# Delta-rule steps of a vision tower: two half-width read sums joined into one

## The chip, the cores and the metric

The kernel runs on one core of a Trainium2 chip. It is written instruction by instruction: each of TensorE (PE), VectorE (DVE), ScalarE (ACT), GpSimd (POOL) and the queue of SyncE (SP) has its own program, and semaphores order them against each other. The metric is the device time of one execution in microseconds, taken as the median of several.

## The reference

The model is a vision tower of four blocks over 32 images of 64 tokens with 256 features. The change lies in the attention of the second block, a gated delta rule with 16 heads of 16 features, which runs over the 64 tokens one after the other:

```
q = silu(x @ Wq); k = silu(x @ Wk); k = k * rsqrt(sum(k * k, -1) + 1e-12); v = x @ Wv
beta = 2 * sigmoid(x @ Wbet); a = sigmoid(x @ Wf)
def step(S, inp):                                   # S: 16 x 16 for each image and head
    qt, kt, vt, at, bt = inp
    Sd = at[..., None, None] * S
    u = vt - einsum('bhk,bhkv->bhv', kt, Sd)
    Sn = Sd + bt[..., None, None] * kt[..., None] * u[:, :, None, :]
    o = einsum('bhk,bhkv->bhv', qt, Sn)
    return Sn, o
```

Every state needs the one before it. There are 32 x 16 = 512 independent chains of 64 steps. Patch embedding, an attention, a mixture of experts, a channel mixer, a causal attention, grouped experts, a linear recurrence and an int8 projection surround it; the change leaves them alone.

## The kernel before

The 512 chains are laid out as 128 partitions (8 images x 16 heads) by 4 groups `g`. A state is 4 x 16 x 16 = 1024 f32 values on each partition, two PSUM banks. Two copies, `S[0]` (banks 0 and 1) and `S[1]` (banks 2 and 3), are used in turn. `halves[h]` cuts the four groups into two halves of 512 values, one bank each. The loop over `t` is written once on each engine, in `delta_layer`:

- DVE (`vector`, lines 1608 to 1623) does for half 0 and then for half 1: the product of the state with the scaled key (`prod`, line 1613), its sum over the 16 keys (`read`, line 1616), the subtraction from the value (`u`, line 1619), and the outer product of the scaled key with `u` (`outer`, line 1622). `prod` and `outer` lie in the tile that the trace calls `made`; `read` and `u` lie in PSUM bank 4. All four are written for both halves before the next `t` begins.
- ACT (`scalar`, from line 1511) waits for `prod_made{h}` and fades the state of half h into the other copy with two instructions (line 1517, `faded{h}`). It then copies the present state of that half to SBUF for the output (`copy_out`, line 1494). After both halves it stores an earlier output (line 1498).
- PE (`add_outer`, line 1411) waits for `faded{h}` and `outer_made{h}` and adds the outer product to the faded state with a matmul by the identity; the semaphore `state{h}` tells DVE that this half of the next state is there. After both halves PE sums the folded output products of step t - 2 (`sum_folded`, line 1419, four matmuls of 64 columns), and sometimes squares (line 1426).
- POOL (`gpsimd`, from line 1669) multiplies the copied state with the query for the output (line 1674) and folds it twice (line 1678). It waits for both copies of a step (`state_copied`).

An f32 matmul shows in the trace as two MATMUL instructions, so a "pair" below is one call of `add_outer` for one half.

The loop keeps two things going at once: while PE adds the outer product of one half, DVE works on the other half. The wait that joins them is this one, at the head of each half:

```
dve.wait_ge(sem(f"state{h}"), t + 1)
```

Nothing else in the block is queued behind the loop until it ends. Its last output, a short tail of normalisation, and the loads for the next layers follow.

Of the kernel before, what the change touches and what calls it, by code (L numbers as in the profile page):

```python
# [13 lines left out]
ALU = mybir.AluOpType  # L14
ACT = mybir.ActivationFunctionType
AX = mybir.AxisListType
# [57 lines left out]
def bcast(ap, axis, n):  # L74

    ap = ap.unsqueeze(axis)
    shape = [int(s) for s in ap.shape]
    shape[axis] = n
    return ap.to_broadcast(shape)
# [1172 lines left out]
def delta_layer(nc, sem, io, banks, H, ident, minus_half, token_rows, gate, chains, rates, front, chain, all_sent,  # L1252
# [15 lines left out]
    q, k, v, o = (chain[n] for n in "qkvo")  # L1268
    ka, kb, qt = (chain[n] for n in ("ka", "kb", "q_by_time"))
    rate, n2, rn, tmp, f = (chain[n] for n in ("rate", "n2", "rn", "rn_tmp", "f"))  # L1270
    states = "p n m -> p (n m)"

    def by_state(ap):
        return ap.rearrange("p (g v k) -> p g v k", g=CG, v=HD)

    Sc = [by_state(xT[i][:, :, :].rearrange(states)) for i in range(2)]
    prod, outer = (by_state(made_all[:, 2 * i:2 * i + 2, :].rearrange(states)) for i in range(2))
# [10 lines left out]
    read, u = small[:, 0, :, :], small[:, 1, :, :]  # L1288
    halves = [slice(2 * h, 2 * h + 2) for h in range(2)]
# [249 lines left out]
    def vector(dve):  # L1539
# [68 lines left out]
        for t in range(TOK):  # L1608
            now = slice(t, t + 1)
            for h in range(2):  # L1610
                at = halves[h]
                dve.wait_ge(sem(f"state{h}"), t + 1)
                dve.tensor_tensor(prod[:, at, :, :], S[t % 2][:, at, :, :], bcast(ka[:, t, at, :], 2, HD),  # L1613
                                  ALU.mult).then_inc(sem(f"prod_made{h}"), 1)
                dve.wait_ge(sem(f"prod_made{h}"), t + 1)
                dve.tensor_reduce(read[:, at, :], prod[:, at, :, :], AX.X, ALU.add  # L1616
                                  ).then_inc(sem(f"read_made{h}"), 1)
                dve.wait_ge(sem(f"read_made{h}"), t + 1)
                dve.tensor_tensor(u[:, at, :], v[:, at, :, now].rearrange("p g d o -> p g (d o)"),
                                  read[:, at, :], ALU.subtract).then_inc(sem(f"u_made{h}"), 1)  # L1620
                dve.wait_ge(sem(f"u_made{h}"), t + 1)
                dve.tensor_tensor(outer[:, at, :, :], bcast(kb[:, t, at, :], 2, HD), bcast(u[:, at, :], 3, HD),  # L1622
                                  ALU.mult).then_inc(sem(f"outer_made{h}"), 1)
        for n in range(CHUNKS_O - 1):
# [19 lines left out]
    def gpsimd(pool):  # L1644
# [24 lines left out]
        for t in range(TOK - 1):  # L1669
# [7 lines left out]
            for i, n in enumerate((8, 4)):  # L1677
                pool.tensor_tensor(qs[:, :, :, 0:n], qs[:, :, :, 0:n], qs[:, :, :, n:2 * n],  # L1678
                                   ALU.add).then_inc(sem("qs_folded"), 1)
                pool.wait_ge(sem("qs_folded"), 2 * t + i + 1)  # L1680

    return {"early_loads": early_loads, "sync": sync, "tensor": tensor, "scalar": scalar, "vector": vector,
            "gpsimd": gpsimd}

# [1012 lines left out]
```

## Time and profile before

| | |
|---|---|
| median of 3 runs | 1444.47 us (1439.58 to 1448.13) |
| profiled execution, its time | 1432.16 us |
| its span, first to last instruction | 1430.5 us |
| busy in the span: PE / DVE / ACT / POOL | 80% / 58% / 40% / 40% |
| mean granted TensorE clock | 0.917 of full speed |
| loop over the tokens | from 679.6 us to about 976 us of the span |

Busy shares are over the whole span, which has stages with quite different limits. The loop is one of these stages, a fifth of the time. In it no DMA of any size runs, and what matters is how the four engines pass a state round within a step.

### The profile page before, as it was taken

Reading aid. Unit: us, or ns where it says so; the run is one execution under the profiler, and the core shown is the slowest. Engines: PE = TensorE matmul, PEld = TensorE weight load, DVE = VectorE, ACT = ScalarE, POOL = GpSimd, SP = SyncE. Lnnn points to the kernel's source line nnn. Section 1 sums busy time; section 2 is a strip of 40 time slices with the busy share of each in tenths; the row PEclk is TensorE's granted clock in tenths of the full one; section 3 lists DMA queues with packets and bytes.
Section 4 is the critical chain, followed back from the end, with each engine's and each line's share of the span. In section 5 each row is a group of like instructions: output and inputs, shape, how many; then the busy total and the mean of one; then the engine's idle time right before and its main releaser. Section 6 shows DMA issues by size and latency. Waiting matters only on the chain. (4 is left out here: it accounts for less than half of the span.)

```text
span 1430.5 us, 24008 instructions
## 1 busy us (share of the span) xinstructions
PE 1137.5 (80%) x8723; PEld 838.7 (59%) x8723; DVE 833.5 (58%) x1982; ACT 565.7 (40%) x1340; POOL 566.3 (40%) x626
## 2 busy tenths in 40 slices
PE   5999984699999999686776777764899999776843
PEld 3666663687988889532333444442677777654532
DVE  3666665311121211455999999996477777522875
ACT  1455541211111112154566666662234443334643
POOL 0111111232323333343799999994121122120756
PEclk9999995799999999799799999997799999978975
DMA  4111100788888887387000000002000040037501
GB/s 133 42 45 35 42 13 17 302 332 341 318 300 316 307 312 269 98 220 179 0 0 1 0 1 0 1 1 74 12 12 9 9 185 2 1 123 250 170 12 49
DMA packets 83349, 162.19 MB, mean 113 GB/s; under 512 B 44128, under 2 KB 62176, under 8 KB 77216
## 3 DMA queue, kind: packets, MB, share of 16 engines
q1 hardware_dynamic: 55536, 111.23, 22.6%
q0 software_dynamic: 10512, 45.10, 8.7%
q10 hardware_dynamic: 17184, 4.33, 1.4%
q8 instruction: 71, 1.16, 0.3%
q14 instruction: 46, 0.38, 0.1%
HBM read 134.28 MB, written 26.35 MB: 112 GB/s over the span
## 5 line engine op out<-in xcount | busy, mean ns | idle before, releaser
L1411 PE MATMUL banks<-made,ident 128*128 128x512 f32 x256 | 151.1, 674 | 90.4 <-DVE made L1622 89.6
L908 PE MATMUL banks<-rowsT,w_up 128*128 128x128 f32 x1716 | 199.8, 276 | 0.7 <-DMA w_up<-in_up_w 0.7
L908 PEld LDWEIGHTS banks<-rowsT,w_up 128*128 128x128 f32 x1716 | 196.4, 193 | 1.3 <-DMA w_up<-in_up_w 1.0
L1674 POOL TENSOR_TENSOR ys<-xT_d,q_by_time 128x1024 f32<-128x1024 f32 x63 | 148.8, 2361 | 17.9 <-ACT xT_d L1494 9.8
L1517 ACT ACTIVATE banks<-banks,rate 128x256 f32<-128x256 f32 x256 | 104.1, 445 | 116.5 <-DVE made L1613 116.5
L1411 PEld LDWEIGHTS banks<-made,ident 128*128 128x128 f32 x256 | 40.9, 201 | 154.2 <-ACT banks L1517 128.2
L1678 POOL TENSOR_TENSOR ys<-ys 128x512 f32<-128x512 f32 x126 | 124.8, 990 | 9.9
L923 PE MATMUL banks<-w_down,hT 128*128 128x256 f32 x468 | 115.1, 388 | 0.6 <-DVE res L1092 0.6
L1082 DVE TENSOR_TENSOR hT<-banks,silu 64x128 f32<-64x128 f32 x39 | 11.0, 283 | 170.7 <-ACT silu L966 170.7
L852 POOL DMA_DIRECT2D w_down<-in_down_w x39 | 22.8, 584 | 195.2 <-PE banks L923 190.1
L1821 POOL TENSOR_TENSOR agg_b<-agg_b,minus_half 128x1 f32<-128x1 f32 x48 | 28.5, 593 | 171.1 <-DVE agg_b L2031 169.9
L923 PEld LDWEIGHTS banks<-w_down,hT 128*128 128x128 f32 x468 | 82.6, 189 | 22.0 <-issue 13.9
L1419 PEld LDWEIGHTS banks<-ys,ident 128*128 128x128 f32 x504 | 73.5, 210 | 35.6 <-issue 33.3
L1616 DVE TENSOR_REDUCE banks<-made 128x32 f32<-128x512 f32 x128 | 89.0, 695 | 4.4
L1622 DVE TENSOR_TENSOR made<-kb,banks 128x512 f32<-128x512 f32 x128 | 88.0, 687 | 4.4
L1613 DVE TENSOR_TENSOR made<-banks,ka 128x512 f32<-128x512 f32 x128 | 87.6, 684 | 3.5 <-POOL kb L1655 2.8
L956 ACT COPY rowsT<-banks 128x256 f32<-128x256 f32 x39 | 14.5, 373 | 156.8 <-PE banks L108 156.8
L1494 ACT COPY xT_d<-banks 128x512 f32<-128x512 f32 x126 | 75.4, 598 | 0.0
L1419 PE MATMUL banks<-ys,ident 128*128 128x64 f32 x504 | 72.0, 300 | 2.2 <-POOL ys L1678 2.2
L1092 DVE COPY res<-banks 128x256 f32<-128x256 f32 x39 | 16.6, 425 | 82.8 <-PE banks L923 82.8
L2430 POOL TENSOR_TENSOR agg<-agg,minus_half 128x1 f32<-128x1 f32 x48 | 31.6, 658 | 68.1 <-DVE agg L2483 67.8
L458 POOL TENSOR_TENSOR ss<-ss,minus_half 128x1 f32<-128x1 f32 x16 | 8.8, 550 | 117.4 <-DVE ss L702 117.4
(316 smaller groups left out, 2352.1 us busy)
## 6 DMA issues: line engine op xcount, KB each, us to landing
w_up<-in_up_w SPq DMA_DIRECT2D x39, 1408.0 KB, 6.3
w_down<-in_down_w POOLq DMA_DIRECT2D x39, 768.0 KB, 5.6
inter<-res_x SPq DMA_DIRECT2D x16, 512.0 KB, 3.0
back<-inter SPq DMA_DIRECT2D x15, 512.0 KB, 3.9
patches<-in_patches SPq DMA_DIRECT2D x16, 384.0 KB, 3.2
f<-in_f SPq DMA_DIRECT2D x6, 1024.0 KB, 10.7
ys<-token_rows SPq DMA_DIRECT2D x16, 256.0 KB, 2.8
xn_rows<-xn_all SPq DMA_DIRECT2D x16, 128.0 KB, 1.7
```

Of the source, the lines that this page charges most:

```text
L908: ins = pe.matmul(out[:, m * P:(m + 1) * P], w[:, c, m * P:(m + 1) * P], x[:, c, :], start=(c == 0), stop=(c == 1))
L923: ins = pe.matmul(Y, hT[j % 2][0:n, c, :], w_down[j % DEEP][0:n, c, :], start=(c == 0), stop=(c == FULL))
L1411: pe.matmul(S[(t + 1) % 2][:, halves[h], :, :], ident[:, :], outer[:, halves[h], :, :], start=False, stop=True, skip_group_check=True).the ...
L1419: ins = pe.matmul(o_sum, ident[:, :], products[t % 2][:, :, :, n], start=(n == 0), stop=(n == 3))
L1494: act.copy(Sc[n % 2][:, halves[h], :, :], S[n % 2][:, halves[h], :, :]).then_inc(sem("state_copied"), 1)
L1517: ins = act.activation(S[(t + 1) % 2][:, g, :, :].rearrange("p v k -> p (v k)"), S[t % 2][:, g, :, :].rearrange("p v k -> p (v k)"), ACT.Copy,
L1613: dve.tensor_tensor(prod[:, at, :, :], S[t % 2][:, at, :, :], bcast(ka[:, t, at, :], 2, HD), ALU.mult).then_inc(sem(f"prod_made{h}"), 1)
L1616: dve.tensor_reduce(read[:, at, :], prod[:, at, :, :], AX.X, ALU.add).then_inc(sem(f"read_made{h}"), 1)
L1622: dve.tensor_tensor(outer[:, at, :, :], bcast(kb[:, t, at, :], 2, HD), bcast(u[:, at, :], 3, HD), ALU.mult).then_inc(sem(f"outer_made{h}"), 1)
L1674: pool.tensor_tensor(qs[:, :, :, :], Sc[(t + 1) % 2][:, :, :, :], bcast(qt[:, t, :, :], 2, HD), ALU.mult).then_inc(sem("qs_made"), 1)
L1678: pool.tensor_tensor(qs[:, :, :, 0:n], qs[:, :, :, 0:n], qs[:, :, :, n:2 * n], ALU.add).then_inc(sem("qs_folded"), 1)
L2430: pool.tensor_tensor(agg[n][t % 2][:, 1:2], agg[n][t % 2][:, 1:2], minus_half[:, 0:1], ALU.pow).then_inc(sem(f"ln{n}_rstd"), 1)
```

## The change: what it does

DVE computes the products of both halves first, then one sum and one subtraction over the full width, and then the two outer products. Per step, two sums of 128x512 become one of 128x1024, and two subtractions of 128x32 become one of 128x64. The semaphores `read_made` and `u_made` are now single. The programs of the other engines are the same.

```diff
@@ -1612,13 +1612,15 @@
                 dve.wait_ge(sem(f"state{h}"), t + 1)
                 dve.tensor_tensor(prod[:, at, :, :], S[t % 2][:, at, :, :], bcast(ka[:, t, at, :], 2, HD),
                                   ALU.mult).then_inc(sem(f"prod_made{h}"), 1)
+            for h in range(2):
                 dve.wait_ge(sem(f"prod_made{h}"), t + 1)
-                dve.tensor_reduce(read[:, at, :], prod[:, at, :, :], AX.X, ALU.add
-                                  ).then_inc(sem(f"read_made{h}"), 1)
-                dve.wait_ge(sem(f"read_made{h}"), t + 1)
-                dve.tensor_tensor(u[:, at, :], v[:, at, :, now].rearrange("p g d o -> p g (d o)"),
-                                  read[:, at, :], ALU.subtract).then_inc(sem(f"u_made{h}"), 1)
-                dve.wait_ge(sem(f"u_made{h}"), t + 1)
+            dve.tensor_reduce(read, prod[:, :, :, :], AX.X, ALU.add).then_inc(sem("read_made"), 1)
+            dve.wait_ge(sem("read_made"), t + 1)
+            dve.tensor_tensor(u, v[:, :, :, now].rearrange("p g d o -> p g (d o)"), read, ALU.subtract
+                              ).then_inc(sem("u_made"), 1)
+            dve.wait_ge(sem("u_made"), t + 1)
+            for h in range(2):
+                at = halves[h]
                 dve.tensor_tensor(outer[:, at, :, :], bcast(kb[:, t, at, :], 2, HD), bcast(u[:, at, :], 3, HD),
                                   ALU.mult).then_inc(sem(f"outer_made{h}"), 1)
```

## Rows read from the trace of the kernel before

**Rows 1.** Page, busy time in 40 slices of 35.8 us.

```profile
PE   5999984699999999686776777764899999776843
DVE  3666665311121211455999999996477777522875
POOL 0111111232323333343799999994121122120756
PEclk9999995799999999799799999997799999978975
```

**Rows 2.** Instructions of line 1613: count, durations, first and last start, who waited.

```profile
L1613 DVE TENSOR_TENSOR made<-banks,ka x128: 683/684/693, 679.6 to 973.6; 128x512 f32<-128x512 f32 x128
...
  ACT banks L1517: 116.5, 125
```

**Rows 3.** Timeline of one step: start us, us, instructions [idle before].

```profile
827.60 2.37 POOL L1674 TENSOR_TENSOR ys<-xT_d,q_by_time 128x1024 f32<-128x1024 f32 x1
827.72 0.68 DVE L1613 TENSOR_TENSOR made<-banks,ka 128x512 f32<-128x512 f32 x1
827.95 1.10 PE L1411 MATMUL banks<-made,ident 128*128 128x512 f32 x2 [1.20 <-DVE made L1622]
828.44 0.81 ACT L1517 ACTIVATE banks<-banks,rate 128x256 f32<-128x256 f32 x2 [0.81 <-DVE made L1613]
828.44 0.69 DVE L1616 TENSOR_REDUCE banks<-made 128x32 f32<-128x512 f32 x1
828.88 1.04 PE L1419 MATMUL banks<-ys,ident 128*128 128x64 f32 x8
829.17 0.60 ACT L1494 COPY xT_d<-banks 128x512 f32<-128x512 f32 x1
829.17 0.23 DVE L1619 TENSOR_TENSOR banks<-chain_v,banks 128x32 f32<-128x32 f32 x1
829.43 0.69 DVE L1622 TENSOR_TENSOR made<-kb,banks 128x512 f32<-128x512 f32 x1
830.04 0.68 DVE L1613 TENSOR_TENSOR made<-banks,ka 128x512 f32<-128x512 f32 x1
830.04 2.06 POOL L1678 TENSOR_TENSOR ys<-ys 128x512 f32<-128x512 f32 x2
830.26 1.10 PE L1411 MATMUL banks<-made,ident 128*128 128x512 f32 x2 [0.34 <-DVE made L1622]
```

**Rows 4.** Timeline of the loop's end, where DVE waits for a state.

```profile
971.26 0.68 DVE L1613 TENSOR_TENSOR made<-banks,ka 128x512 f32<-128x512 f32 x1
...
976.09 1.10 PE L1411 MATMUL banks<-made,ident 128*128 128x512 f32 x2 [0.64 <-DVE made L1622]
...
977.30 1.23 DVE L1629 TENSOR_TENSOR made<-banks,q_by_time 128x1024 f32<-128x1024 f32 x1 [1.07 <-PE banks L1411]
...
978.56 1.22 DVE L1631 TENSOR_REDUCE chain_o<-made 128x64 f32<-128x1024 f32 x1
...
981.67 0.27 ACT L1498 COPY chain_o<-banks 128x64 f32<-128x64 f32 x1 [3.29 <-PE banks L1419]
```

**Rows 5.** Timeline, PE alone: eight MATMULs of 512 columns without a wait.

```profile
620.90 3.62 PE L1376 MATMUL banks<-xT_d,w_delta 128*128 128x512 f32 x8
```

**Rows 6.** Timeline: the first pair, at the low clock.

```profile
682.12 2.05 PE L1411 MATMUL banks<-made,ident 128*128 128x512 f32 x2 [13.22 <-DVE made L1622]
```

**Rows 7.** Timeline, PE alone: a low-clock spell inside the loop.

```profile
837.19 1.63 PE L1411 MATMUL banks<-made,ident 128*128 128x512 f32 x2 [1.20 <-DVE made L1622]
838.61 1.80 PE L1419 MATMUL banks<-ys,ident 128*128 128x64 f32 x8
```

**Rows 8.** Stretches: us, busy PE, PEld, DVE, ACT, POOL, granted clock, DMA.

```profile
691.14:973.56 282.42, 206.76 (x821) 117.90 (x822) 269.18 (x489) 174.48 (x429) 264.87 (x183) 0.95 0.00 1
990.00:1020.00 30.00, 17.52 (x49) 11.99 (x50) 10.37 (x31) 3.83 (x8) 4.64 (x8) 0.56 0.25 78
```

**Rows 9.** Timeline: a DVE operation on 64 values a partition, before the loop.

```profile
671.87 0.23 DVE L1558 TENSOR_TENSOR rn_tmp<-rn 128x64 f32<-128x64 f32 x1
```

## The prediction

> **What bounds the kernel now.** I read the 40 slices first, to find the stage in which the edit lies. In the eight slices from 679 us on DVE stands at 9 tenths, POOL too after the first of them, and PE at 6 or 7 [rows 1]. That is the loop over the tokens, and either DVE or POOL sets its pace. Then I read the instructions of the product line: 128 of them, half 0 of the first step at 679.59 and half 0 of the last at 971.26 [rows 2, 4]. That is 63 periods in 291.67 us, 4.63 us each. Nothing else can run beside this stage on another path: the loop's end is followed by a tail that needs its last state, so each microsecond here is one of the whole.
>
> Within one step [rows 3] DVE runs its eight instructions without a wait. A half is 0.68, then 0.69 after a gap of 0.03, 0.23 after 0.04, 0.69 after 0.03; the next product starts 0.08 before the outer product ends. This makes 2.30 to 2.32 a half and 4.62 a step. The state is never late: the pair of matmuls for half 0 starts at 827.95, ends at 829.05, and its state is wanted at 830.04, that is 0.99 later. In that time DVE works on half 1. So DVE is the pacer, and the two halves hide each other's trip through PE. POOL is close behind: 2.37, a gap of 0.07, and 2.06 for two folds, with 0.07 more before it could start again, are 4.57. ACT waits for DVE each half [rows 2] and PE for the outer product (1.20 and 0.34, rows 3).
>
> **The change part by part.** *Fewer, wider instructions.* The sum over 1024 values a partition has a twin at the loop's end, 1.22 us [rows 4], against twice 0.69: 0.16 less, and a gap of 0.03 less. It writes SBUF there and PSUM here. At half width the sum that writes PSUM takes 0.69, which doubled, 1.38, is the upper bound. I take 1.22, to which it is nearest in size. The subtraction of 64 values: a 64-wide operation takes 0.23 [rows 9] and two half-width ones 0.46 [rows 3]; I take 0.25, as one operand is in PSUM. With the gaps DVE issues about 0.53 less a step: 4 x 0.685 + 1.22 + 0.25 + 0.10 of gaps - 0.24 for three overlaps of 0.08 = 4.07, if it never waits.
>
> *The order.* Now it does wait. Both outer products come at the end of a step, and the next step begins with the product that needs half 0 of the new state. I follow the chain from the start of product 0, at full clock.
>
> - From the end of an outer product to its pair on PE is 0.14 (829.43 + 0.69 = 830.12 to 830.26, rows 3), the pair is 1.10, and from its end to a waiting DVE instruction 0.11 (977.19 to 977.30, rows 4). Together L = 1.35.
> - The pair of half 1 queues behind that of half 0 on PE. Eight MATMULs without a wait take 3.62 in all [rows 5]; with the last one's own length of 592 ns, that is 0.43 from start to start, 0.87 a pair. A pair that other matmuls follow at once holds them off by 0.93 (827.95 to 828.88, rows 3). I take d = 0.90, so product 1 starts 0.90 after product 0. If both pairs paid their full length one after the other, d would be 1.10.
> - From the start of product 1: 0.68 + 0.03 + 1.22 + 0.03 + 0.25 + 0.04 + 0.69 = 2.94 to the end of outer product 0.
>
> A period is d + 2.94 + L = 0.90 + 2.94 + 1.35 = **5.19** instead of 4.63. DVE is idle some 0.74 ahead of product 0 and 0.22 ahead of product 1. Had only DVE's own pace set product 1 (0.60 after product 0), it would be 4.89.
>
> *What is queued behind.* ACT's fade of half 0 starts 0.72 after product 0 and takes 0.81, a copy 0.60, fade 1 again 0.81: it is over some 2.8 after product 0, while PE wants it at 4.6 when outer product 1 is there. So fade and copy stay hidden, with over 1 us of cover. POOL needs 4.57 in 5.19 and gets slack. PE's sums of folded products (1.04) run after both pairs in DVE's long stretch and are over before the next outer product. The tail gains a little: the last POOL product waits for the copy of half 1, which now ends 3.4 after product 0 of its step against 4.35 (975.61 to 971.26), less 0.2 for PE then: 0.8 us less, once [rows 4].
>
> *The clock.* At the low clock (1.2 GHz, half of 2.4) a pair takes 2.05 [rows 6]. Today that costs nearly nothing, since 0.99 of slack takes it: a spell at 837 stretches a pair to 1.63 and the sums to 1.80 [rows 7], and the periods stay near 4.62. In the new order each such step pays: L = 2.30 and d = 1.80, a period of 7.04. What share s of the time is low? Now the granted clock is 0.95 [rows 8], so s = 0.1 (two levels, 1 and 0.5), with PE busy 73% in that row. At full clock the new step has PE busy about 1.10 + 0.90 + 0.87 = 2.87 of 5.19, 55%, with one idle piece of 2.3 us where now there are pieces of 1.20 and 0.34. The nearest stretch with so little, 58% busy, was granted 0.56, s = 0.88 [rows 8]. Against that end: a new step wholly at the low clock has PE busy about 2.05 + 1.80 + 1.60 = 5.45 of 7.04, 77%, more than the 73% of today's loop, which mostly has the full clock; so it would not stay low. I take s = 0.3 as an estimate between the two, nearer today's loop because instructions and cycle are the same. The mean period is 1 / (0.3/7.04 + 0.7/5.19) = 5.63.
>
> The Trainium skill (TensorE: Matmul & The Clock Gate, HAM oscillation) says that matmuls in bursts with waits between them make the clock fall again and again. This trace agrees that bursts go with a low clock [rows 8]; by it s would lie above today's, by an amount the page does not give for this case.
>
> The Trainium skill (Perfetto Trace Analysis, Optimizing Scalar/DVE Operations) says that grouping operations helps a saturated engine, and that breaking them up helps where the engine makes others wait. The first half would give the third rival below its gain, the second speaks against this change.
>
> **The sum.** 63 x (5.63 - 4.63) = +63, less 0.8: **+62 us**. Against the profiled execution's own 1432.2 (span 1430.5) that is 1494. The median of the runs stands 12 above that execution; the same +62 on 1444.5 gives **1506.5**.
>
> **The rivals.**
>
> 1. *The clock falls for most of the loop.* s from 0.5 to 0.88: periods 5.97 to 6.75, +84 to +133, 1528 to 1577. For it: the 58% row. Against it: 77% busy when low.
> 2. *The wait is shorter than worked out.* Product 1 is not held by PE's second pair (4.89) and the clock is as good as full: (4.89 - 4.63) x 63 = +17, up to +35 for the full chain at full clock: 1461 to 1479. For it: parts of the matmul ends in a profile are modelled. Against it: the 1.07 wait in rows 4 is measured on DVE.
> 3. *The other side: DVE stays the pacer.* If the new state were ready when DVE asks, the period would be DVE's 4.07, floored by POOL's 4.57: 63 x -0.06 = -4 us, 1441, no change; if POOL too were faster than I read, 63 x -0.56 = -35, 1409. The point from which it decides: L + d must be under 4.63 - 2.94 = 1.69, and the rows give 2.25. Only if the pair took 0.5 instead of 1.10 would it hold.
>
> **How the numbers follow.** The forecast, s from 0.1 to 0.5 (+43 to +84), has 0.74; rival 1 0.12; rival 2 0.09; rival 3 0.05, of which I give 0.02 to faster and 0.03 to no change. About 0.5% (7 us) is what a measurement of this kernel tells from no change. All of the rest is slower: 0.95. The range reaches down to the full chain at full clock throughout, 1444.5 + 34 = 1478, and 4 below it, the upper part of rival 2 (a d of 1.10 would move it up by 13, a sum at its upper bound by 10): 1474. It reaches up to s = 0.6, +96, with the 10 of that bound on it, the lower half of rival 1: 1550. Left out are rival 3 (0.05), some 0.07 of rival 2 and 0.05 of rival 1.
>
> **What would show it right or wrong.** In the profile after: product lines for half 0 should start 5.2 apart at full clock and about 7 in a low spell, with the first 679.6 unmoved; DVE should wait for PE's line 1411 twice a step, 0.7 and 0.2 at full clock; the wide sum should be near 1.22 and the subtraction 0.25; PE's wait for outer product 0 should be one of some 2.3 us a step; POOL should show idle time that it doesn't have now; the clock over the loop should be 0.75 to 0.95. The prediction fails if DVE shows no wait for PE (rival 3), if product 1 follows product 0 without a gap (rival 2), if ACT's fades appear as the last releaser of PE for either half, which would add to 5.19, or if the clock is under 0.75 (rival 1).

## The result and the profile after

The changed kernel takes 1560.9 us, median of 4 runs (1559.4 to 1564.0); the kernel before took 1445.7, median of 4. The ratio is 1.081, with a 95% interval of 1.077 to 1.085. That is 115 us slower, where +62 was forecast and a range of 1474 to 1550 given. The sign was right and the size was not. Every ratio here leaves out executions more than 1.5% above the fastest of their kernel, which are one of the first experiment (2407 us beside three of 1471 to 1475) and three of the sixth (1515 to 1522 beside three of 1489 to 1497), while every median has all of them.

The slices of the page of the changed kernel, each 38.9 us, show the stage from 679 us on grown from eight to nearly eleven slices. DVE and POOL, which stood at 9 [rows 1], stand mostly at 6, and the granted clock, 7 to 9 there before, is at 6 to 8:

```profile
PE   5999973999999996846667766766489999878753
DVE  3666664111211226466666666666557777622775
POOL 0111102223333324346666766766212121101556
PEclk9999975999999997967777667668689999959875
```

The instructions of the product line answer to [rows 2]. The loop starts at the same time. DVE now waits for PE 126 times, which it never did before:

```profile
L1613 DVE TENSOR_TENSOR made<-banks,ka x128: 678/691/693, 679.4 to 1091.3; 128x512 f32<-128x512 f32 x128
  PE banks L1411: 138.0, 126
```

Half 0 of the last step starts at 1090.44 (the last row of the loop, 1091.3, is half 1), so 63 periods take 411.0 us: 6.52 each instead of 4.63, or 119 us in all. This accounts for the whole change in the medians. The rest of the profiled difference (span 1557.7 against 1430.5) is 8 us after the loop; over all kernels of this study that part varied between 456 and 470 us with no edit in it.

The stretch of these periods on all engines (us, busy PE, PEld, DVE, ACT, POOL, granted clock, DMA) answers to [rows 8]. The clock is 0.72: 56% of the time at the low one of its two levels.

```profile
679.50:1090.40 410.90, 280.07 (x817) 158.69 (x818) 262.37 (x378) 178.11 (x439) 265.93 (x184) 0.72 0.00 0
```

I read the start of every product 0 from the timeline. The 63 periods fall into three kinds, with some in between: 7 of 5.18 us, 12 of 6.97 to 7.01, and 31 of 6.81 to 6.91. The timeline of the changed kernel shows one step of each kind. First, one at the full clock:

```profile
852.02 1.95 PE L1411 MATMUL banks<-made,ident 128*128 128x512 f32 x4 [1.04 <-DVE made L1624]
853.16 0.69 DVE L1613 TENSOR_TENSOR made<-banks,ka 128x512 f32<-128x512 f32 x1 [0.68 <-PE banks L1411]
853.82 1.04 PE L1419 MATMUL banks<-ys,ident 128*128 128x64 f32 x8
854.01 0.69 DVE L1613 TENSOR_TENSOR made<-banks,ka 128x512 f32<-128x512 f32 x1 [0.17 <-PE banks L1411]
854.68 1.26 PE L1426 MATMUL banks<-w_delta,ident 128*128 128x72 f32 x10
854.81 1.23 DVE L1617 TENSOR_REDUCE banks<-made 128x64 f32<-128x1024 f32 x1
856.07 0.27 DVE L1619 TENSOR_TENSOR banks<-chain_v,banks 128x64 f32<-128x64 f32 x1
856.37 1.28 DVE L1624 TENSOR_TENSOR made<-kb,banks 128x512 f32<-128x512 f32 x2
```

The reader sees the chain as one piece: both pairs of matmuls run back to back (1.95 for the four MATMULs), product 1 starts 0.85 after product 0, then follow the wide sum, the subtraction and the outer products. The next product 0 comes at 858.34. Here PE also has the squares of line 1426 to do; five of the seven steps of this kind have them. Next, a step at the low clock, where the pairs take 3.75 and the sums 1.81:

```profile
873.16 3.75 PE L1411 MATMUL banks<-made,ident 128*128 128x512 f32 x4 [1.62 <-DVE made L1624]
876.71 1.81 PE L1419 MATMUL banks<-ys,ident 128*128 128x64 f32 x8
880.14 3.75 PE L1411 MATMUL banks<-made,ident 128*128 128x512 f32 x4 [1.63 <-DVE made L1624]
```

And one of the commonest kind. The pairs, on which DVE waits, take 3.59; the sums, on which the next product doesn't wait, run at the full clock in 1.05:

```profile
804.24 3.59 PE L1411 MATMUL banks<-made,ident 128*128 128x512 f32 x4 [2.35 <-DVE made L1624]
806.32 0.69 DVE L1613 TENSOR_TENSOR made<-banks,ka 128x512 f32<-128x512 f32 x1 [1.63 <-PE banks L1411]
807.67 1.05 PE L1419 MATMUL banks<-ys,ident 128*128 128x64 f32 x8
811.09 3.58 PE L1411 MATMUL banks<-made,ident 128*128 128x512 f32 x4 [2.37 <-DVE made L1624]
```

Half of such a step is at the full clock, but in the wrong half. It lasts 6.8 us, nearly as long as a step wholly at the low clock. Five stretches show the clock beside it (one common step, then its first and its second half, then two low steps, and nearly two full ones):

```profile
804.20:811.00 6.80, 4.48 (x12) 2.37 (x12) 4.14 (x7) 2.84 (x7) 4.30 (x4) 0.75 0.01 2
804.20:807.50 3.30, 3.26 (x4) 1.51 (x5) 1.18 (x2) 0.46 (x2) 3.14 (x3) 0.50 0.02 5
807.60:810.90 3.30, 1.11 (x9) 0.86 (x7) 2.86 (x5) 2.29 (x6) 0.96 (x2) 1.00 0.00 0
873.00:887.00 14.00, 10.71 (x24) 6.26 (x24) 8.36 (x14) 5.66 (x14) 8.69 (x7) 0.50 0.00 1
852.00:862.00 10.00, 7.83 (x44) 5.67 (x44) 7.96 (x12) 5.43 (x14) 7.97 (x7) 1.00 0.01 2
```

One thing holds for all 63 steps. From the start of one step's pairs to the start of the next, take off the time of the four MATMULs, and 3.22 to 3.26 us are left, whatever the clock: 5.18 - 1.95, 6.82 - 3.59, 6.98 - 3.75. So the clock costs this loop only what it adds to the pairs.

### The profile page after: what moved, and what is told of

It reads as the page before. It is cut to its first block and busy times, and to the rows that moved or that the text cites. A ratio compares the mean times of both kernels' runs of the same rounds, so it can differ in the third digit from the quotient of the medians.

```text
span 1557.7 us, 23944 instructions
## 1 busy us (share of the span) xinstructions
PE 1214.1 (78%) x8723; PEld 886.9 (57%) x8723; DVE 817.8 (53%) x1854; ACT 565.3 (36%) x1340; POOL 565.2 (36%) x626
## 5 line engine op out<-in xcount | busy, mean ns | idle before, releaser
L1411 PE MATMUL banks<-made,ident 128*128 128x512 f32 x256 | 209.5, 966 | 142.4 <-DVE made L1624 142.4
L1411 PEld LDWEIGHTS banks<-made,ident 128*128 128x128 f32 x256 | 67.7, 292 | 213.1 <-issue 213.1
L1419 PEld LDWEIGHTS banks<-ys,ident 128*128 128x128 f32 x504 | 85.2, 237 | 54.3 <-issue 30.3
L1624 DVE TENSOR_TENSOR made<-kb,banks 128x512 f32<-128x512 f32 x128 | 82.2, 683 | 2.2
L1617 DVE TENSOR_REDUCE banks<-made 128x64 f32<-128x1024 f32 x64 | 78.5, 1227 | 6.6
L1419 PE MATMUL banks<-ys,ident 128*128 128x64 f32 x504 | 77.8, 313 | 1.1 <-POOL ys L1680 1.1
L466 PE MATMUL banks<-w_tok,patches 128*128 128x256 f32 x192 | 51.3, 406 | 2.5 <-DVE k_cols L755 2.5
```

Source lines behind the costliest of these rows:

```text
L466: ins = pe.matmul(X, patches[t % SLOTS_IN][:, c, :], w_tok[:, c, :], start=(c == 0), stop=(c == PC - 1), skip_group_check=True)
L1411: pe.matmul(S[(t + 1) % 2][:, halves[h], :, :], ident[:, :], outer[:, halves[h], :, :], start=False, stop=True, skip_group_check=True).the ...
L1419: ins = pe.matmul(o_sum, ident[:, :], products[t % 2][:, :, :, n], start=(n == 0), stop=(n == 3))
L1617: dve.tensor_reduce(read, prod[:, :, :, :], AX.X, ALU.add).then_inc(sem("read_made"), 1)
```

## The experiments

The theory after the result, theory A in the expectations: the new order makes the trip through PE part of every step (5.18 us at the full clock), and low-clock spells, let in by PE's long idle piece, do the rest. The main rivals were that the clock has nothing to do with PE's idle time, and that the wide instructions themselves are the cost. Each kernel was timed beside the kernel before on the same chip; the ratios are to that.

**Extra matmuls in PE's idle piece.** At the end of each step of `tensor`:

```diff
+            for _ in range(6 if t < 62 else 0):
+                pe.matmul(banks[:, 7, 256:384], ident[:, :], ident[:, :], start=True, stop=True,
+                          skip_group_check=True)
```

In this kernel and the next, the extra matmuls of steps 60 and 61 share a bank with the sum of squares of the third stretch of tokens and disturb it, so that their output is wrong, while the work of a step is the one described. In the later kernels the extra matmuls stop at step 59.

> The changed kernel with six extra 128-column f32 matmuls by the identity on TensorE at the end of each step up to the 62nd, into an unused part of PSUM bank 7; nobody waits for them. Theory A (the serial chain costs 5.18 us a step at the full clock, and the rest of the slowdown comes from low-clock spells that the long idle piece of TensorE lets in): the clock over the loop rises from 0.73 to 0.95 or more, periods are 5.2 and the loop's 63 periods about 327 us instead of 411, so the whole is about 1445 + 35 = 1480 us. Rival B (the low clock does not depend on what TensorE does in its idle time, and the period is set by the order alone): the extra matmuls change nothing or hold up the pairs, 1560 us or more, clock near 0.73.

Measured: 1474.7 us, ratio 1.023 (1.014 to 1.032). The stretch of its 63 periods:

```profile
680.50:1009.00 328.50, 269.11 (x1561) 199.05 (x1562) 262.29 (x378) 172.81 (x439) 267.09 (x184) 0.99 0.00 1
```

After the first two, nearly every period is 5.18 or 5.19, 5.21 in the mean. PE does more work and the kernel is 86 us faster than the changed one. So the low clock came from what PE did, and it cost that much. Rival B is out. The edit makes the idle piece shorter (from some 2.3 us to 1.00) and PE busier (82% of the loop instead of 68%) at once, and so can't say which of the two counts. The timeline of its PE shows the filled gap (line 1451) ahead of the pairs:

```profile
826.16 1.95 PE L1411 MATMUL banks<-made,ident 128*128 128x512 f32 x4
827.96 1.04 PE L1419 MATMUL banks<-ys,ident 128*128 128x64 f32 x8
828.82 1.53 PE L1451 MATMUL banks<-ident 128*128 128x128 f32 x12
831.35 1.96 PE L1411 MATMUL banks<-made,ident 128*128 128x512 f32 x4 [1.00 <-DVE made L1627]
```

**The same in the kernel before.**

> Control: the kernel before with the same six extra matmuls a step up to the 62nd. TensorE has some 1.5 us idle a step there, and the extra work takes about 1.3 us. Theory A: the clock goes from 0.95 to 1.0, but the periods stay at 4.61 since VectorE paces them and low-clock spells are absorbed by 0.99 us of slack: between 0 and 3 us faster than before. If the extra matmuls hold up a pair by more than the slack, it is slower by up to 0.3 us a step, 20 us. Rival B: no difference in the clock.

Measured: 1441.2 us, ratio 1.000 (0.997 to 1.003), clock 0.99 over the loop. Nearly all periods stay between 4.60 and 4.63; eight, around the steps with squares, grow to between 5.07 and 5.80. The full clock brings the old order nothing, as the slack of [rows 3] had it. The extra matmuls are no gain in themselves.

**The order without the merging.** In `vector`, three loops over the halves take the place of the wide instructions:

```diff
-            dve.tensor_reduce(read, prod[:, :, :, :], AX.X, ALU.add).then_inc(sem("read_made"), 1)
...
+            for h in range(2):
+                at = halves[h]
+                dve.wait_ge(sem(f"prod_made{h}"), t + 1)
+                dve.tensor_reduce(read[:, at, :], prod[:, at, :, :], AX.X, ALU.add
+                                  ).then_inc(sem(f"read_made{h}"), 1)
...
```

> The new order without the merging: both products, then two half sums, two half subtractions, two outer products, each half-width as before. Theory A (the order costs, the merging saves a little): the chain from product 1 to the end of outer product 0 grows by a sum and a subtraction, 0.69 + 0.03 + 0.22 less 0.53 for the shorter first sum and less 0.04: about 0.15 to 0.4 us a step more than the changed kernel, 1565 to 1590 us, if the clock behaves alike. Rival C (the wide instructions themselves are what costs, because they delay the first half): the time falls back towards before, under 1500 us.

Measured: 1525.8 us, ratio 1.059 (1.050 to 1.067). This is less than the changed kernel, against my expectation: the merging costs time. The mean period is 6.01, with a clock of 0.71. At the full clock this kernel has periods of 4.86, at the low clock 6.66, both 0.32 less than with the wide instructions. The DVE rows of a step here, and then of the changed kernel, say why:

```profile
883.81 0.69 DVE L1613 TENSOR_TENSOR made<-banks,ka 128x512 f32<-128x512 f32 x1 [1.01 <-PE banks L1411]
884.41 1.27 DVE L1618 TENSOR_REDUCE banks<-made 128x32 f32<-128x512 f32 x2
885.60 0.34 DVE L1623 TENSOR_TENSOR banks<-chain_v,banks 128x32 f32<-128x32 f32 x2
885.85 1.27 DVE L1628 TENSOR_TENSOR made<-kb,banks 128x512 f32<-128x512 f32 x2
```

```profile
814.71 0.69 DVE L1613 TENSOR_TENSOR made<-banks,ka 128x512 f32<-128x512 f32 x1 [0.85 <-PE banks L1411]
815.50 1.23 DVE L1617 TENSOR_REDUCE banks<-made 128x64 f32<-128x1024 f32 x1
816.76 0.27 DVE L1619 TENSOR_TENSOR banks<-chain_v,banks 128x64 f32<-128x64 f32 x1
817.06 1.28 DVE L1624 TENSOR_TENSOR made<-kb,banks 128x512 f32<-128x512 f32 x2
```

Two half sums in a row take 1.27, hardly more than one wide sum of 1.23, since the second doesn't depend on the first and their ends overlap. And the first half sum begins 0.60 after product 1 begins, before that product is over, while the wide sum must wait for it and begins 0.79 after. The next two instructions start earlier as well, by 0.07 and 0.05. From product 1 to outer product 0 it is 2.04 here and 2.35 there.

**The sums of folded products ahead of the pairs.**

```diff
         for t in range(TOK):
-            add_outer(t)
             if t >= 2:
                 sum_folded(t - 2)
+            add_outer(t)
```

> The changed kernel with one edit on TensorE: the sums of folded products stand ahead of the pairs of a step instead of behind them, the same work. Theory A in its sharper form (what counts is where in the step TensorE idles, and where the spells fall on the pairs): the idle time is cut into two pieces and the time changes by more than 10 us, most likely down, 1500 to 1550 us, with the clock above 0.73. Rival D (only the total busy share of TensorE counts): the clock stays at 0.73 and the time within 5 us of 1561.

Measured: 1584.0 us, ratio 1.103 (1.092 to 1.113). It moved by more than 10 us, but upward, and it does not answer its question. At the full clock the sums wait for ACT's store (a wait of 1.70 on line 1498), end up right ahead of the pairs and hold them off: the shortest period is 5.61 instead of 5.18. The idle time was not cut in two. That adds 0.43 in the two steps that have the full clock. The mean period grew by 0.45 (6.97 against 6.52) with the clock where it was, but how the rest of the steps come to it is not shown: 28 of them lie between 7.0 and 7.1, and six at 7.85 or more.

**The order alone, with the extra matmuls.** The kernel of the third experiment with the lines of the first, up to step 59.

> The new order with half-width sums and subtractions, plus six extra matmuls a step up to the 60th. Theory A (each step has a fixed chain, and the clock only adds to it): all periods become the 4.86 us that the same order shows without the extra matmuls at the full clock, loop 63 x 4.86 = 306 us, the whole about 1441 + 15 = 1456 us. The difference to the merged kernel with extra matmuls (1475) is then the price of the merging alone, 0.32 us a step. Rival E (without them the two differ only by where the clock falls, and the instructions cost alike): 1475 us as well.

Measured: 1455.5 us, ratio 1.011 (1.008 to 1.014), clock 0.99. Most periods are 4.86, 4.91 in the mean. With the clock taken out, the order costs 17 us by the medians and the merging another 19 (the first experiment has 1475); by the ratios it is 15 and 18.

**Half as many extra matmuls** in the changed kernel:

```diff
-            for _ in range(6 if t < 62 else 0):
+            for _ in range(3 if t < 60 else 0):
```

> The changed kernel with three extra matmuls a step (0.7 us) up to the 60th instead of six. Theory A (the clock holds once the idle piece is short enough): between 1475 and 1561 us, or already 1475 if half the work is enough; clock over the loop between 0.73 and 1.0. It tells how much of the idle piece matters; a time above 1561 would speak against the theory.

Measured: 1505.7 us, ratio 1.036 (1.032 to 1.041), with runs from 1489 to 1522. The profiled one took 1521 and is among the longest; how the shorter ones divide their steps, no trace shows. Its first 25 periods are long, nearly all of them the 6.82 of the common kind, and most of the later ones 5.19. The same instructions a step run in either way. Two stretches, and the step at which it changes:

```profile
683.40:848.00 164.60, 120.55 (x408) 70.28 (x409) 100.97 (x146) 68.24 (x167) 99.40 (x69) 0.74 0.00 0
852.00:1054.00 202.00, 147.93 (x760) 102.13 (x759) 158.25 (x228) 105.45 (x268) 164.11 (x115) 0.97 0.00 1
```

```profile
850.82 3.59 PE L1411 MATMUL banks<-made,ident 128*128 128x512 f32 x4 [1.67 <-DVE made L1627]
854.25 1.04 PE L1419 MATMUL banks<-ys,ident 128*128 128x64 f32 x8
855.11 1.48 PE L1426 MATMUL banks<-w_delta,ident 128*128 128x72 f32 x12
856.43 0.88 PE L1451 MATMUL banks<-ident 128*128 128x128 f32 x6
857.64 1.96 PE L1411 MATMUL banks<-made,ident 128*128 128x512 f32 x4 [0.33 <-DVE made L1627]
```

The squares fill the gap for three steps, the pairs after them find the full clock, and it mostly stays (0.97 in the second stretch). The changed kernel leaves its long periods at the same steps (periods 26 to 29 and 44 to 47 are 5.2 to 5.9), but falls back afterwards.

**Only the products first.** One part of the order: both products, then for each half its sum, subtraction and outer product. Against the kernel before it is two lines:

```diff
                                   ALU.mult).then_inc(sem(f"prod_made{h}"), 1)
+            for h in range(2):
+                at = halves[h]
                 dve.wait_ge(sem(f"prod_made{h}"), t + 1)
```

> One part of the change alone: both products first, then for each half its sum, subtraction and outer product as before. Theory A: product 1 waits for the state of half 1, whose pair can start only after the last outer product; from the start of product 1 to the end of outer product 1 is 3.85 us, with 1.35 for the trip through TensorE 5.20 us a period at the full clock and 6.15 at the low clock. The pairs are apart again, so the clock should be near 0.9: mean 5.3 us, 1441 + 43 = 1484 us, 1475 to 1510. Rival C (only the late outer product 0 costs): half 0 hides the trip of half 1 and the time stays at 1441.

Measured: 1518.1 us, ratio 1.054 (1.049 to 1.058). Rival C is out: it is product 1, moved ahead, that brings the wait. The periods are 5.12 at the full clock and mostly 6.20 at the low one (some are 6.80), near the 5.20 and 6.15 worked out, but the clock was 0.65 and the mean 6.04. At the full clock the pairs are apart; at the low clock they mostly run back to back again. My guess of 0.9 failed just as the 0.85 behind the prediction had.

This kernel also speaks against the simple form of theory A. Without the first step, PE idles 1.22 us a step here and 1.21 in the kernel before, and the longest idle piece of a step is 1.07 and 1.01 in the mean; yet the clock over the loop is 0.65 here and 0.93 there. In its steps at the full clock without squares PE does idle more, 0.48 and 1.57 of 5.12 us against 1.20 and 0.34 of 4.6, so a spell may begin in idle time. But what holds it is not idle time that the profile shows: two steps of 6.20, in which PE is busy 86% of the time and never idle for longer than 0.85, lie wholly at the low clock:

```profile
717.60:730.00 12.40, 10.71 (x24) 6.16 (x25) 8.78 (x17) 5.64 (x14) 8.71 (x7) 0.50 0.00 0
```

**The chain made longer.** The changed kernel with the subtraction written twice:

```diff
-            dve.wait_ge(sem("u_made"), t + 1)
+            dve.wait_ge(sem("u_made"), 2 * t + 1)
+            dve.tensor_tensor(u, v[:, :, :, now].rearrange("p g d o -> p g (d o)"), read, ALU.subtract
+                              ).then_inc(sem("u_made"), 1)
+            dve.wait_ge(sem("u_made"), 2 * t + 2)
```

> The changed kernel with the subtraction done twice, 0.30 us more on the chain of each step. In the changed kernel 36 of 63 periods are between 6.81 and 6.86 us, with the low clock on the pairs alone. Theory G (in these plateaus the period is locked to the clock's own rhythm, and work on the chain is absorbed): the plateau stays at 6.82, only full-clock periods grow from 5.18 to 5.48 and low ones from 6.98 to 7.28, the whole is at most 8 us slower than the changed kernel, 1555 to 1569. Rival H (the chain's length adds up in every step): +0.30 x 63 = 19 us, 1580 us, and plateaus at 7.12.

(The count in it is too high: 29 periods of the changed kernel lie between 6.81 and 6.86, and two more up to 6.91.) Measured: 1569.2 us, ratio 1.090 (1.086 to 1.094). That is 8 us above the changed kernel by the medians and 0.9% of 1440, 13 us, by the ratios. The whole time falls between the two theories; the loop decides. Its 63 periods take 430.8 us instead of 411.0, near the 19 more of rival H, and what comes after them was 10 us shorter, within the spread that it has without any edit. The mean period is 6.84, that is 0.31 more. The row of equal periods is gone: nearly all now lie spread between 6.3 and 7.3. Theory G falls: the long row of 6.82 absorbed nothing, and in the mean a longer chain adds up. Rival H's row at 7.12 did not come either. The clock went from 0.72 to 0.65.

**Less work for the engines that pace the loop before.** If DVE's 4.61 and POOL's 4.57 are the bound before [rows 3], taking work from both should make a faster kernel, and from one alone nearly nothing. The value becomes a 17th column of the product tile, written by ACT, and the key factor is negated:

```diff
-                dve.tensor_reduce(read[:, at, :], prod[:, at, :, :], AX.X, ALU.add
-                                  ).then_inc(sem(f"read_made{h}"), 1)
-                dve.wait_ge(sem(f"read_made{h}"), t + 1)
-                dve.tensor_tensor(u[:, at, :], v[:, at, :, now].rearrange("p g d o -> p g (d o)"),
-                                  read[:, at, :], ALU.subtract).then_inc(sem(f"u_made{h}"), 1)
+                dve.wait_ge(sem(f"value_in{h}"), t + 1)
+                dve.tensor_reduce(u[:, at, :], prod[:, at, :, :], AX.X, ALU.add
+                                  ).then_inc(sem(f"u_made{h}"), 1)
```

For POOL, the second fold goes, and PE sums eight slices, four after each pair:

```diff
-            for i, n in enumerate((8, 4)):
-                pool.tensor_tensor(qs[:, :, :, 0:n], qs[:, :, :, 0:n], qs[:, :, :, n:2 * n],
-                                   ALU.add).then_inc(sem("qs_folded"), 1)
-                pool.wait_ge(sem("qs_folded"), 2 * t + i + 1)
+            pool.tensor_tensor(qs[:, :, :, 0:8], qs[:, :, :, 0:8], qs[:, :, :, 8:16],
+                               ALU.add).then_inc(sem("qs_folded"), 1)
+            pool.wait_ge(sem("qs_folded"), t + 1)
```

> A version of the kernel before, in its order, that takes work from the engines that pace it. The value enters the product tile as a 17th column, written by ScalarE, and the key factor is negated, so that one sum gives u and the subtraction is gone. GpSimd folds once instead of twice, and TensorE sums eight slices instead of four, in two portions between the pairs. If VectorE paces the loop before with GpSimd just behind: VectorE needs 0.68 + 0.03 + 0.73 + 0.03 + 0.69 - 0.08 = 2.08 a half, 4.16 a step, GpSimd 3.8; 63 x (4.16 - 4.63) = -30 us, 1411 us. Rival F (something else, TensorE's or ScalarE's order, is as near): 1430 us or more.

> Only one part of the faster version: the value as a 17th column of the product tile, the subtraction gone, GpSimd's folds as before. If GpSimd's own 4.57 us a step stands right behind VectorE's 4.61: period 4.57, 2 to 4 us faster than before, 1436 us, with GpSimd never idle and VectorE waiting. Rival: GpSimd was not near, period 4.16 and 1411 us.

> Only the other part: GpSimd folds once, TensorE sums eight slices in two portions between the pairs; VectorE as before. If VectorE paces: period 4.61, within 3 us of before, 1438 to 1442 us. Rival: GpSimd paced, and the time falls by more than 10 us.

Measured: both together 1413.5 us, ratio 0.983 (0.977 to 0.988); the value column alone 1435.3, ratio 0.997 (0.994 to 1.000); one fold alone 1434.5, ratio 0.996 (0.993 to 0.999). The two single ones are hardly told from no change; the periods tell more. The mean periods are 4.23, 4.56 and 4.61. With the value column alone the single periods jump between 4.17 and 5.5 (two are longer), yet their mean is POOL's own 4.57. Two engines paced the loop before, as read. The version with both beats both kernels; its DVE rows:

```profile
820.80 0.68 DVE L1638 TENSOR_TENSOR made<-banks,ka 128x512 f32<-128x512 f32 x1
821.52 0.73 DVE L1642 TENSOR_REDUCE banks<-made 128x32 f32<-128x544 f32 x1
822.28 0.69 DVE L1645 TENSOR_TENSOR made<-kb,banks 128x512 f32<-128x512 f32 x1
822.89 0.68 DVE L1638 TENSOR_TENSOR made<-banks,ka 128x512 f32<-128x512 f32 x1
```

A half is 2.09 here against 2.30, and PE, busy 94% of the loop, has a clock of 0.98.

## Why the prediction was right or wrong

**Right: what bounds the loop before.** DVE paces it with POOL just behind; relieving both gave 25 us, relieving one 4 or 5 (of the loop's own time 25.4, and 4.1 or 1.2).

**Right: the chain of the new order.** d was 0.85 to 0.86 for my 0.90, the wide sum 1.23 for 1.22, the subtraction 0.27 for 0.25. Two gaps were off: between product 1 and the sum it is 0.10 and not 0.03, and between the end of the first pair and product 0 it is 0.03 and not 0.11 (858.31 to 858.34). So the step at the full clock is 0.85 + 3.05 + 1.28, where I had 0.90 + 2.94 + 1.35. The errors cancel: the period is 5.18 for the forecast 5.19, an agreement to 0.01 that is partly luck. The low one is 6.98 for 7.04. (In the part on DVE's own pace, 4.62 less 4.07 is 0.55 and not 0.53; nothing hangs on it.) With the clock held up, the kernel costs 34 us, the +34 named for the full clock throughout. ACT's fades stayed hidden, POOL got its slack, DVE waited twice a step. Rivals 2 and 3 are out.

**Wrong: the share s of the low clock, and with it the mean period.** I took s = 0.3; it was 0.56. That put the result into rival 1, which had been given 1528 to 1577 us and a chance of 0.12. Three things in that step failed:

1. The argument that held s down. I worked out that PE would be busy 77% of a step at the low clock, more than today's 73%, and so would not stay there. It was busy 77% (10.71 of 14.00 us) and stayed, for up to five periods in a row and 12 in all; with only the products first it stayed at 86%. A busy share at the low clock can't be set against one at the full clock, since the same work counts for nearly twice the time (a step's pairs 3.75 instead of 1.95). The nearest row, 58% busy at a clock of 0.56 [rows 8], was the better guide.
2. The mean. The formula spreads the low clock evenly over a step. With s = 0.56 it gives 1 / (0.56/6.98 + 0.44/5.18) = 6.05, and 6.52 was measured. Only the pairs carry the clock into the period, and in half of the periods the spell lay on them, and the full clock on the sums and the idle piece. Such a step has the low clock for half its time and pays 1.64 of the 1.80 us that a wholly low one pays. Of the 1.34 us a step that the clock costs in the mean, 0.87 are the evenly spread share and 0.47 this coincidence; the prediction had 0.44 in all.
3. The reason for staying near today's value, that instructions and cycle are the same. What differs is how PE's work lies in a step. The first experiment shows that filling PE's idle time brings the full clock back, but no run separates the length of the idle piece from the total of PE's work: the fourth was meant to and did not, and with only the products first PE's idle time a step, as the profile shows it, was that of the kernel before and the clock 0.65. So this part of the step stays open.

The Trainium skill (TensorE: Matmul & The Clock Gate, HAM oscillation) describes bursts of matmuls with waits between them, waits for transfers there, after which the clock is low again and again. The trace agrees as to the direction: the clock was 0.72 in the loop with a long wait a step, here a wait for DVE, and 0.99 with the wait filled. I had let it shift s only a little.

**Wrong in its parts, though the sum held: that merging saves.** I counted 0.16 and 0.21 us less for the wide instructions and then lost them in the chain. Measured against the same order with half-width instructions, merging adds 0.32 a step. I had doubled the duration of single instructions, while two independent ones in a row overlap: two half sums take 1.27 and not 1.38, two subtractions 0.34 and not 0.46. Nor had I seen that a half sum can start before the other half's product is over.

So the 119 us of the loop divide as follows, over 63 periods: 15 for the order (4.63 to 4.86), 20 for the merging (to 5.18), 84 for the clock (to 6.52). The split between the last two is the one at the full clock. With the clock as it was granted the merging cost more, 0.51 a step (6.52 against 6.01 for the order alone), since the clock's own part is 1.15 a step there and 1.34 here.

**Open.** What in PE's work brings the low clock, why the spell settles on the pairs in 31 periods, and why the clock returns for good in one kernel and falls back in another after the same squares, is described here and not explained. The one idea that was tried, that the period locks and absorbs work, fell.

## What to carry to other kernels

Where a recurrence passes through two engines, two halves in turn are what hides the trip; an edit that saves instructions but makes both halves wait at one place puts the whole trip into every step. Once matmuls are on the chain, ask what TensorE's idle time will do to the granted clock: price the step at both clocks, and give a case of its own to the low one falling on the chain's own matmuls, since an even spread was 0.47 us a step too low here. Before merging two independent instructions on VectorE, look at what they take in a row, not at twice one of them.

## What was not expected of the hardware

- Extra matmuls that nobody needs made a kernel 86 us faster, 1561 to 1475, by holding the granted clock at 0.99 instead of 0.72. In the kernel before, with its 0.99 us of slack, they changed nothing (ratio 1.000).
- One program has two ways to run the same step: with three extra matmuls a step, 24 periods of 6.7 to 6.9 us were followed mostly by periods of 5.19 in one execution. Its executions spread over 34 us, and only that one was traced.
- The low clock stayed on with PE busy 77% of the time (10.71 of 14.00 us), and, with only the products first, 86% (10.71 of 12.40), while the loop before had a clock of 0.95 at 73%.
- Two independent subtractions of 128x32 in a row take 0.34 us, though one by itself takes some 0.21.
